# Order of the mixing matmuls in the two stages of the first graph layer: one behind each of the first four transposed projections, in place of all four behind the first

## What is computed

```python
def _L0_gnn_ref(h, adj, W_left, W_right, W_lin, b_lin, ln_a, ln_b):
    for l in range(2):
        m_left  = einsum('bsh,oh->bso', h, W_left[l])
        m_right = einsum('bsh,oh->bso', h, W_right[l])
        u_left  = einsum('bih,bjh->bij', h, m_left) / temper
        u_right = einsum('bih,bjh->bij', h, m_right) / temper
        u = u_left * triu(adj, 0) + u_right * swapaxes(triu(adj, 1), 1, 2)
        e = exp(u) * adj
        attention = e / (sum(e, axis=2) + 1e-10)
        h_lin = einsum('bsh,oh->bso', h, W_lin[l]) + b_lin[l]
        ctx = matmul(attention, h_lin)
        h = relu(layer_norm(ctx, ln_a[l], ln_b[l]))
    return h          # x = x + this
```

## Time and profile before

| | |
|---|---|
| median of 3 runs | 3472.05 us (3471.08 to 3472.71) |
| the profiled execution | 3472.62 us, span 3470.8 us |
| TensorE matmuls | 3094.8 us, 89% of the span |
| TensorE weight loads | 2569.0 us, 74% |
| VectorE | 2376.4 us, 68% |
| ScalarE | 1164.1 us, 34% |
| GpSimd | 1094.8 us, 32% |
| granted TensorE clock, mean | 0.962 |

### The profile page before, as it was taken

One profiled execution on the slowest core, in us unless ns is written; L12 is line 12 of the kernel. 1 busy time (PEld: TensorE's weight loads), 2 busy tenths in 40 slices (PEclk: granted clock), 3 DMA queues, 4 the chain that ended last, 5 costly groups with the idle time before them and its releaser, 6 DMA issues. The chain is left out here.

```text
span 3470.8 us, 63460 instructions
## 1 busy us (share of the span) xinstructions
PE 3094.8 (89%) x21632; PEld 2569.0 (74%) x21632; DVE 2376.4 (68%) x4488; ACT 1164.1 (34%) x2145; POOL 1094.8 (32%) x909
## 2 busy tenths in 40 slices
PE   6999979999588888888899998999994888988887
PEld 5888868888466666766788887888883677777776
DVE  4445445455578888787677775677776788888887
ACT  2433423332244444443222222221121344444443
POOL 1222224544333333333111110333332333333333
PEclk9999989999799999998999998999997999999999
DMA  3222233233101111111211113222222010111000
GB/s 89 65 83 63 65 108 109 91 96 113 56 21 40 39 39 39 39 39 51 61 54 59 59 50 121 65 86 86 86 84 64 21 40 20 39 39 39 27 22 30
DMA packets 197099, 208.30 MB, mean 60 GB/s; under 512 B 72736, under 2 KB 197024, under 8 KB 197024
## 3 DMA queue, kind: packets, MB, share of 16 engines
q1 hardware_dynamic: 197024, 207.33, 19.4%
HBM read 131.80 MB, written 75.50 MB: 60 GB/s over the span
## 5 line engine op out<-in xcount | busy, mean ns | idle before, releaser
L931 PE MATMUL psum<-fast 128*128 128x384 f32 x3456 | 650.8, 342 | 19.3 <-issue 7.8
L931 PEld LDWEIGHTS psum<-fast 128*128 128x128 f32 x3456 | 599.2, 189 | 48.3 <-DVE room L1325 14.8
L1325 DVE TENSOR_TENSOR room<-psum,rows 128x384 f32<-128x384 f32 x640 | 352.1, 555 | 400.7 <-PE psum L931 170.9
L693 PE MATMUL psum<-fast 128*128 128x512 f32 x1728 | 458.8, 419 | 99.8 <-DVE fast L1307 89.5
L693 PEld LDWEIGHTS psum<-fast 128*128 128x128 f32 x1728 | 332.9, 199 | 194.5 <-issue 108.7
L752 PE MATMUL psum<-fast 128*128 128x512 f32 x1728 | 417.9, 399 | 16.4 <-DVE fast L1307 16.4
L752 PEld LDWEIGHTS psum<-fast 128*128 128x128 f32 x1728 | 326.9, 190 | 91.4 <-issue 17.2
L569 POOL TENSOR_TENSOR room<-room 64x768 f32<-64x768 f32 x128 | 234.9, 1835 | 446.8 <-DVE room L1402 229.5
L1086 ACT ACTIVATE room<-psum 128x512 f32<-128x512 f32 x384 | 215.5, 594 | 454.6 <-PE psum L830 453.8
L559 POOL TENSOR_TENSOR room<-room 128x768 f32<-128x768 f32 x128 | 188.5, 1473 | 469.7 <-DVE room L1390 265.0
L830 PE MATMUL psum<-mask,room 128*128 128x128 f32 x1536 | 222.6, 284 | 50.9 <-ACT room L1086 24.9
(11 more groups left out here) (108 smaller groups left out, 4919.5 us busy)
## 6 DMA issues: line engine op xcount, KB each, us to landing
x_ring<-x_mid SPq DMA_DIRECT2D x64, 768.0 KB, 4.6
x_mid<-x_ring SPq DMA_DIRECT2D x48, 768.0 KB, 3.9
x_ring<-x_in SPq DMA_DIRECT2D x32, 768.0 KB, 4.6
z_mid<-x_ring SPq DMA_DIRECT2D x32, 768.0 KB, 4.1
z_sb<-z_mid SPq DMA_DIRECT2D x32, 768.0 KB, 5.9
adjc<-adj SPq DMA_DIRECT2D x96, 128.0 KB, 3.9
out<-x_ring SPq DMA_DIRECT2D x16, 768.0 KB, 3.9
w_raw<-w_all SPq DMA_DIRECT2D x19, 576.0 KB, 4.3
```

The source lines that it names most:

```text
L693: mm = nc.tensor.matmul(dst, wpart[m][:, c, oc * P:(oc + 1) * P], hpart[:, c, :], start=(k == 0), stop=(k == 3 * C - 1))
L931: mm = nc.tensor.matmul(dst[:, 0:H], hpart[G.par][:, c, t * P:(t + 1) * P], wpart[m][:, c, :], start=(k == 0), stop=(k == 3 * C - 1))
L1325: done(nc.vector.tensor_tensor(dst, src, rows[:, m], ALU.add), "evac_n")
```

## The change

`mix(g, t)` goes behind `part(g + 1, t)` for each t, and the remaining projections follow from part 4 on. The waits stay with their pieces, and the program of every other engine is the same.

```diff
                     def body(g, one, two):
-                        if one:
-                            part(g + 1, 0)
                         for t in range(T):
+                            if one:
+                                part(g + 1, t)
                             mix(g, t)
                         if one:
-                            for j in range(1, 2 * C + 1):
+                            for j in range(T, 2 * C + 1):
                                 part(g + 1, j)
                             score(g + 1)
```

## The result

The changed kernel takes **3613.2 us** (median of 4 runs, 3611.18 to 3614.86) against 3472.38 for the kernel before: ratio 1.0406, 95% interval 1.0388 to 1.0424, so 141 us or 4.1% slower. The forecast was 3592 us, in a range of 3556 to 3630. The profiled execution has a span of 3609.4 us.

What follows compares the result with a forecast made beforehand. Both stages were taken as bound by TensorE's own stream. Waits of 98 us plus 22 us of clock falls gave 120 us on the profiled 3472.6 us, so 3592 us against the median, range 3556 to 3630.

Steps and rivals of the forecast that it cites:

- Mixing 0 to 2: First three mixing matmuls of each group come 0, 2.04 and 4.08 us later; their VectorE readers are idle otherwise: no cost.
- switching kinds: Three more switch pairs between mixing and projections per group on TensorE: taken as nothing, worst case 17 us.
- The wait of projection 5: TensorE's projection 5 waits for ScalarE's eviction 3, late behind the last mixing matmul's chain: 2.9 or 3.05 us a group.
- what is late next: Further TensorE waits per group: scores 0.15 us in the first stage, second batch of transposes 0.45 us in the second.
- The clock: New TensorE stalls in both stages lower the granted clock in some groups: 22 us.
- 0.6 of 30, eighteen falls: Share of the 30 new stalls in both stages after which the clock falls, taken from 8 of 14 last-stage stalls.
- The price of a fall: Loss per clock fall in the two stages: 1.5 us less the 0.15 or 0.45 us wait absorbed, so 1.2 us.
- the second rival: The clock falls in every group of both stages: 3607 to 3622 us; chance 0.18.
- the faster one: Mixing matmuls hide weight loads behind projections and the wait is covered: 22 us gained, 3450 us; chance 0.02.
- No change: Eviction 3 passes the scaled outputs on ScalarE, or projection 5 does not wait for it: 3472 us; chance 0.02.
- The case in which the clock never falls: Projection 5's wait appears in both stages but the clock stays up: 3570 us; chance 0.12.
- the fifth: The chain from the last mixing matmul is longer than carried over, 1 us a group more: 3622 us; chance 0.08.

Runs made afterwards that it cites:

- k = 1: Kernel before with mixing 0 to 2 behind projection part 0 and the last mixing matmul behind part 1; 3471.9 us, ratio 1.000.
- k = 3: Kernel before with mixing 0 to 2 behind projection part 0 and the last mixing matmul behind part 3; 3613.4 us, ratio 1.0406.
- the control with ScalarE's new order: Kernel before, TensorE's order kept, ScalarE evicting parts 3 and 4 before the scaled outputs and 5 before the last two; 3532.7 us, ratio 1.0175.
- the filler: The changed kernel plus nine matmuls into an unused bank ahead of projection 5 in each group; 3571.4 us, ratio 1.0284.
- the first experiment: The changed kernel with ScalarE evicting parts 3 and 4 before the scaled outputs and part 5 before the last two; 3547.8 us, ratio 1.0221.
- delayed copies: Kernel before with four idle ScalarE copies ahead of eviction 3, first stage only: 960 elements (2.22 us wait) 3520.2 us; 1152 elements (2.86 us) 3536.7 us.
- both orders changed: The changed kernel with ScalarE's evictions 3 and 4 before the scaled outputs and VectorE's part 6 eviction before the additions; 3534.6 us, ratio 1.0179.
- four fillers: The changed kernel plus four matmuls that compute nothing used, ahead of projection 5 in each group; 3605.2 us, ratio 1.0378.
- the split scores: Kernel before with the last quarter of the scores moved between the second and third batch of transposes; 3521.0 us, ratio 1.0141.
- k = 2: Kernel before with mixing 0 to 2 behind projection part 0 and the last mixing matmul behind part 2; 3510.5 us, ratio 1.011.

## Why the prediction was right, and where its sizes were off

*What bounds the stages*: TensorE's stream. This fits k = 1, where a piece moves, no wait comes, and the time stays. In the second stage the other engines are busy up to 53% of TensorE's time, not "half of that or less"; nothing hangs on it.

*Mixing 0 to 2 cost nothing, and switching kinds costs nothing*: confirmed. k = 3 with the first three at their old place and the change with them spread are equal to 0.2 us in the median. A projection with its mixing matmul takes 2.72 us against 2.70, which is 0.02 us for a pair of switches.

*The wait of projection 5*: forecast 2.9 us (3.05 in the second stage) plus 0.15 (0.45) for what is late next, 98 us in all. Measured in groups without a fall 3.29 and 3.23 us, 98 us in all. The sum is right, but two of its parts were off and cancelled, and that is luck. The next waits hardly came: none of the scores, 0.2 us of the transposes. In their place the wait itself was longer than 2.9 us. The chain that sets it was carried over rightly: from the start of the last statistics (L1503) to the end of shift and scale (L1524) it takes 2.8 and 3.0 us in turn, before and after (309.91 to 312.92 above is a long one). What was left out is small and comes every group: in the first stage ScalarE starts 0.27 or 0.22 us behind VectorE's last step and not 0.12, and projection 5, once it starts, takes 2.18 us to the next part (580.63 - 578.45) instead of 2.04 even where the clock does not fall; the spread mixing matmuls add 4 x 0.02 us:

```profile
578.45 2.34 PE L752 MATMUL psum<-fast 128*128 128x512 f32 x9 [2.87 <-ACT room L1131]
580.63 1.75 PE L756 MATMUL psum<-fast 128*128 128x384 f32 x9
```

The idle time that the profile was to show, 85 us in 30 waits, came as forecast (84.9); it is less than what the waits cost.

*The clock*: this is the term that was mis-sized, 22 us against 41 to 43. The step "0.6 of 30, eighteen falls" failed: 28 of 30 fell. I took the share from fourteen waits of 2.75 us in the last stage, where 8 fell, and the waits here are hardly longer (2.61 to 3.04 us idle, 2.83 on average). The share of one stage did not carry over to another: the control with ScalarE's new order waits 2.74 us in its second stage, and there 13 of 14 fell. The price of a fall, 1.2 us, was too low as well: it is some 1.5 us, since the wait that it was to absorb was not there. So the case that I had put at 0.58, eighteen falls, did not come. It was nearly the second rival, put at 0.18 (a fall in every group, 3607 to 3622), and the forecast's range held because it had been drawn wide enough for that rival. The periods show the same: 30.6 to 30.9 us in every group of the first stage, where 29 to 30.6 were named.

The Trainium skill's section "HAM oscillation — how this bites in real kernels" in "TensorE: Matmul & The Clock Gate" had the pattern that came here, throttled again in every round of the loop (28 of 30). It does not carry over to the last stage (8 of 14) or to waits of 1.0 us and less (none of 60), and the page, whose kernel waits longer, does not say that it should.

*The rivals*: the faster one needed hidden weight loads, but a mixing matmul with its projection did not get shorter. "No change" needed something other than eviction 3 to release projection 5; the row names line 1131. The case in which the clock never falls was brought about by the filler, at 3571 us, where the prediction had 3570 for it. A chain that is longer by 1 us a group, the fifth, did not come either: it is as long as before.

## What to carry to other kernels

If a chain hangs on a whole batch of pieces, spreading them over the engine that bounds the kernel makes the chain as late as its last piece. Read who stands behind the end of that chain in the in-order queues of the other engines, and how much of the bound engine's work is left to cover it. Here three of four pieces could move for nothing and the fourth had slack for one projection, not for three. A stall of TensorE that comes back every group has to be priced with the clock: here it added 42 us to some 98. Where such a stall can't be removed, matmuls that compute nothing of use can still pay: nine of them in it saved 42 us here, four of them 8.

## What the hardware showed that I had not expected

- Whether the clock falls is not told by the length of the wait alone. By idle time and falls: 3.1 to 3.3 us in the first experiment's second stage, 14 of 14; 2.6 to 3.0 us in the change, 28 of 30; 2.86 us with delayed copies, 15 of 15; 2.75 us in the last stage, 8 of 14, and 2.74 us in the control's second stage, 13 of 14; 2.22 us with delayed copies, 9 of 15; 2.1 to 2.3 us with both orders changed, 11 of 14; 1.7 to 2.1 us with four fillers, 23 of 30; 1.8 us with the split scores, 4 of 14, and 1.2 to 1.3 us there, none of 14; 0.6 to 1.0 us with k = 2 or nine fillers, none of 60. None of those up to 1.3 us brought a fall; from 1.7 us on the counts do not follow the length, and equal waits in equal surroundings differ (the 2.22 us ones). What decides among them was not settled.
- A fall cost nearly the same wherever it was measured here: 1.46 us with delayed copies, some 1.5 in the change, 1.52 in the attention stage.
- More work for TensorE made the kernel 42 us faster (3613.2 to 3571.4 us).
- VectorE's copy of 512 columns took 1.24 us instead of 0.42 beside GpSimd's elementwise work, in the run with both orders changed.
